# One start block with partition-ordered inputs, and routing sums by four column groups, in a two-expert-layer transformer kernel

## The reference, cut to what matters

```python
pooled = x.mean(axis=1)                 # x is the layer norm here; mean over 256 tokens
h = jnp.tanh(pooled @ W1 + b1)          # 128 -> 32
logits = h @ W2 + b2                    # 32 -> 8 zones
probs = softmax(logits); top_p, top_i = top_k(probs, 3)
...
z = gelu(x @ Wa[e]) @ Wb[e]             # Wa: 8 x 128 x 512, Wb: 8 x 512 x 128
return x + zone_outputs
```

## Time and profile before

| | us |
|---|---|
| median of 3 runs (lowest, highest) | 1666.61 (1665.81, 1667.47) |
| the profiled execution | 1665.73 |
| its span, first to last instruction | 1663.9 |
| `zones` "a" starts (first ACT instruction, L878) | 139.10 |
| `route` "b" starts (first PE instruction, L674) | 1024.73 |
| `zones` "b" starts | 1061.78 |

### The profile page before, as it was taken

One profiled execution on the slowest core, in us unless ns is written; L12 is line 12 of the kernel. 1 busy time (PEld: TensorE's weight loads), 2 busy tenths in 40 slices (PEclk: granted clock), 3 DMA queues, 4 the chain that ended last, 5 costly groups with the idle time before them and its releaser, 6 DMA issues. The chain is left out here.

```text
span 1663.9 us, 43913 instructions
## 1 busy us (share of the span) xinstructions
PE 1475.9 (89%) x14442; PEld 1086.5 (65%) x14443; DVE 1215.6 (73%) x2671; ACT 967.9 (58%) x1459; POOL 464.0 (28%) x672
## 2 busy tenths in 40 slices
PE   0068999998799999999999997899999979799797
PEld 0056999997456666666666656799999834499443
DVE  0755888887577887878778771388888879588695
ACT  0104666664366666666666653366666569677597
POOL 5032121211212222222222211121222168422386
PEclk9999999999799999999999997699999989899899
DMA  8000000000000000000000000000000000000011
GB/s 218 3 1 1 1 0 0 0 0 1 1 2 3 2 0 0 0 0 0 0 0 0 2 2 1 1 0 0 0 0 0 1 1 0 1 1 0 1 44 57
DMA packets 20585, 14.36 MB, mean 9 GB/s; under 512 B 7296, under 2 KB 16416, under 8 KB 20512
## 3 DMA queue, kind: packets, MB, share of 16 engines
q1 hardware_dynamic: 16008, 13.14, 2.8%
q10 hardware_dynamic: 3192, 0.15, 0.2%
q0 software_dynamic: 1312, 0.09, 0.1%
HBM read 9.18 MB, written 4.19 MB: 8 GB/s over the span
## 5 line engine op out<-in xcount | busy, mean ns | idle before, releaser
L1317 DVE TENSOR_REDUCE neg_max<-splat_fill_ps 128x2 f16<-128x512 f32 x512 | 333.8, 691 | 89.8 <-PE splat_fill_ps L1104 86.1
L1244 ACT ACTIVATE splat_probs<-splat_ring 128x1024 f32<-128x1024 f32 x256 | 248.1, 1021 | 98.1 <-PE splat_ring L1131 98.1
L889 ACT ACTIVATE zones_a_hidden<-zones_a_hidden_ps,gelu_scale 128x1024 f32<-128x1024 f32 x96 | 107.0, 1114 | 85.0 <-PE zones_a_hidden_ps L819 83.7
L1131 PE MATMUL splat_ring<-splat_queries,splat_keys 32*128 32x256 f32 x2048 | 152.7, 393 | 4.1 <-ACT splat_probs L1244 3.2
L889 ACT ACTIVATE zones_b_hidden<-zones_b_hidden_ps,gelu_scale 128x1024 f32<-128x1024 f32 x96 | 106.9, 1114 | 84.8 <-PE zones_b_hidden_ps L819 83.4
L1104 PE MATMUL splat_fill_ps<-splat_keys,splat_queries 32*128 32x256 bf16 x1024 | 146.2, 278 | 6.1 <-DVE neg_max L1317 3.2
L1145 PE MATMUL splat_mixed_ps<-splat_probs,values 128*32 128x256 f32 x2048 | 137.0, 385 | 0.4 <-ACT splat_probs L1244 0.4
L938 DVE SCALAR_TENSOR_TENSOR zones_a_hid_lo<-zones_a_hidden,unit_scale,zones_a_hid_hi 128x1024 f16<-128x1024 f32 x96 | 123.6, 1288 | 3.4
L938 DVE SCALAR_TENSOR_TENSOR zones_b_hid_lo<-zones_b_hidden,unit_scale,zones_b_hid_hi 128x1024 f16<-128x1024 f32 x96 | 123.6, 1288 | 3.4
L1131 PEld LDWEIGHTS splat_ring<-splat_queries,splat_keys 32*128 32x128 f32 x2048 | 99.6, 184 | 11.4 <-ACT splat_probs L1244 4.0
L817 PE MATMUL zones_a_hidden_ps<-zones_a_norm_hi,wa_hi 128*128 128x256 f16 x384 | 105.5, 275 | 0.3 <-DVE zones_a_norm_lo L928 0.3
(11 more groups left out here) (357 smaller groups left out, 3482.0 us busy)
## 6 DMA issues: line engine op xcount, KB each, us to landing
out<-x_res SPq DMA_DIRECT2D x16, 256.0 KB, 2.3
stage_a<-L_ffn_Wa SPq DMA_DIRECT2D x1, 2048.0 KB
qkv_rows<-L_attn_qkv_w SPq DMA_DIRECT2D x1, 192.0 KB
attn_w<-L_attn_W SPq DMA_DIRECT2D x1, 192.0 KB
deltas<-L_attn_splat_deltas ACTq DMA_DIRECT2D x6, 0.5 KB
log_scales<-L_attn_splat_log_scales POOLq DMA_DIRECT2D x6, 0.5 KB, 5.3
centers<-L_attn_splat_centers SPq DMA_DIRECT2D x6, 0.5 KB
log_amps<-ttn_splat_log_amplitudes SPq DMA_DIRECT2D x6, 0.5 KB
```

Source lines behind the costliest of these rows:

```text
L889: nc.scalar.activation(hidden[k][:, :, :], hidden_ps[of][:, :, :], ACT.Gelu_apprx_tanh, scale=s.gelu_scale[:, :]).then_inc(gelu_done, 1)
L1131: last = nc.tensor.matmul(ring[g // 2][:, 2 * (g % 2) + key_tile, :], keys[at][rows, t, key_tile * P:(key_tile + 1) * P], queries[at][rows ...
L1244: nc.scalar.activation(probs[u % PROB_BUFFERS][:, :, :, :].rearrange("p h k i -> p (h k) i"), ring[u % 2][:, :, :], ACT.Exp).then_inc(exp_ ...
L1317: nc.vector.tensor_reduce(s.neg_max[:, tile, t:t + 2, GROUP * g + SPLATS], fill_ps[f % 2][:, :, :], AX.X, ALU.max, negate=True).then_inc(m ...
```

## The change

The host now lays the inputs out by partitions: all small weights in one table of 128 rows of 1,680 f32 (0.86 MB), Wa and Wb as 128 rows of 16 KB each, x as 128 rows of 32 KB. Seven transfers, all from SP, replace the former ones: table, Wa, Wb, then x in four pieces. The four blocks in front of `route` "a", and its statistics and sums, become one block `start`. Constants `neg_max` and `values` are filled by POOL in place of DVE. The high parts of the weights are made by ACT (three passes over 4,096 columns), the low parts by DVE, but for a quarter of Wb's, which POOL makes.

The routing sums turn round: x streams (128 columns), and a 128 x 32 matrix that has `rstd` in the sample's own column and zeros elsewhere is the weight; tile n goes to the column group n mod 4, so that 32 rows of output per group collect 16 tiles. The four groups are added by a product with `own_spline` in `route`. For `route` "b" these sums stand at the end of `splat_attention`'s block, and POOL writes `rstd` to one more place per sample.

```diff
+def sum_rows(nc, s, out, samples):
+    for b in samples:
+        for t in range(TILES):
+            n = TILES * b + t
+            g = n % HEAD_GROUPS
+            last = nc.tensor.matmul(out[g * SAMPLES:(g + 1) * SAMPLES, :],
+                                    s.spread_rstd[:, t, SAMPLES * b:SAMPLES * (b + 1)], s.x_res[:, n, :],
+                                    start=(n < HEAD_GROUPS), stop=(n >= SAMPLES * TILES - HEAD_GROUPS))
+    return last
...
+            def _(sp):
...
+                sp.dma_start(s.packed[:, :], a["table"]).then_inc(packed_loaded, 16)
+                sp.dma_start(s.stage_a[:, :], a["wa"]).then_inc(a_loaded, 16)
+                sp.dma_start(s.stage_b[:, :], a["wb"]).then_inc(b_loaded, 16)
+                for n in range(PIECES):
+                    load_rows(n)
...
+            def _(pool):
...
+                nc.gpsimd.memset(s.spread_rstd[:, :, :], 0.0).then_inc(blank, 1)
+                nc.gpsimd.memset(s.neg_max[:, :, :, :], 0.0)
+                nc.gpsimd.memset(s.values[:, :, :, :, 0:SUM_COLUMN + 1], 1.0)
+                nc.gpsimd.memset(s.values[:, :, :, :, SUM_COLUMN + 1:GROUP], 0.0)
+                pool.wait_ge(blank, 1)
+                for n in range(PIECES):
+                    moments.power(pool, n)
+                    if n == 0:
+                        pool.wait_ge(high_ready, 1)
+                        nc.gpsimd.tensor_tensor(s.wb_lo[:, 0:LOW_SPLIT], s.stage_b[:, 0:LOW_SPLIT],
+                                                s.wb_hi[:, 0:LOW_SPLIT], ALU.subtract)
...
+                for n in range(PIECES):
+                    pe.wait_ge(moments.rstd_ready, n + 1)
+                    last = sum_rows(nc, s, sums_ps, range(n * SAMPLES // PIECES, (n + 1) * SAMPLES // PIECES))
+                last.then_inc(sums_done, 1)
...
+                act.wait_ge(scale_ready, 1)
+                nc.scalar.activation(s.stage_b[:, :], s.stage_b[:, :], ACT.Copy,
+                                     scale=scale[:, 1:2]).then_inc(scaled_ready, 1)
+                act.wait_ge(scaled_ready, 1)
+                nc.scalar.activation(s.wb_hi[:, :], s.stage_b[:, :], ACT.Copy).then_inc(high_ready, 1)
+                nc.scalar.activation(s.wa_hi[:, :], s.stage_a[:, :], ACT.Copy,
+                                     scale=scale[:, 0:1]).then_inc(high_ready, 1)
+                act.wait_ge(sums_done, 1)
+                nc.scalar.activation(s.sum_rows[:, :], sums_ps[:, :], ACT.Copy)
...
+                for n in range(PIECES):
+                    dve.wait_ge(x_loaded[n], 16)
+                    moments.statistics(dve, n)
+                dve.wait_ge(high_ready, 2)
+                nc.vector.scalar_tensor_tensor(s.wa_lo[:, :], s.stage_a[:, :], scale[:, 0:1], s.wa_hi[:, :],
+                                               ALU.mult, ALU.subtract)
+                nc.vector.tensor_tensor(s.wb_lo[:, LOW_SPLIT:], s.stage_b[:, LOW_SPLIT:], s.wb_hi[:, LOW_SPLIT:],
+                                        ALU.subtract)
...
 def route(nc, s, stage):
+                nc.tensor.matmul(pooled_ps[:, :], s.sum_rows[:, :], s.own_spline[:, :], start=True, stop=False)
                 pe.wait_ge(products_ready, 1)
...
 def splat_attention(nc, s, stage):
                 run(pe, slot)
+                pe.wait_ge(exp_done, HEAD_UNITS * SAMPLES)
+                for first, end in ((0, SAMPLES - 3), (SAMPLES - 3, SAMPLES)):
+                    pe.wait_ge(ended.ready, end)
+                    last = sum_rows(nc, s, ring[0][:, 0, 0:P], range(first, end))
+                last.then_inc(sums_done, 1)
...
                 run(act, slot)
+                act.wait_ge(sums_done, 1)
+                nc.scalar.activation(s.sum_rows[:, :], ring[0][:, 0, 0:P], ACT.Copy)
...
-                    nc.gpsimd.tensor_copy(s.rstd[:, columns], ended.rstd[at][:, :]).then_inc(ended.ready, 1)
+                    nc.gpsimd.tensor_copy(s.rstd[:, columns], ended.rstd[at][:, :])
+                    own = b * (SAMPLES + 1)
+                    own = slice(own, own + 1) if isinstance(b, int) else bass.ds(own, 1)
+                    nc.gpsimd.tensor_copy(s.spread_rstd[:, :, own],
+                                          ended.rstd[at][:, :].unsqueeze(2)).then_inc(ended.ready, 1)
```

More of the change, by code:

```diff
@@ new lines, with unpack @@
+PACKED_COLUMNS = sum(math.prod(shape) for _, shape in PACKED)
+def unpack(s, table):
+    at, parts = 0, {}
+    for name, shape in PACKED:
+        columns = math.prod(shape)
+        part = table[:, at:at + columns]
+        parts[name] = part if len(shape) == 1 else part.rearrange("p (a b) -> p a b", a=shape[0])
+        at += columns
+    s.qkv_rows, s.out_rows, s.centers, s.deltas = (parts[n] for n in ("qkv_rows", "out_rows", "centers", "deltas"))
+    s.log_scales, s.log_amps, s.movement, s.temperature = (
+        parts[n] for n in ("log_scales", "log_amps", "movement", "temperature"))
+    s.spline_bin, s.knot_b1, s.knot_w2, s.relu_scale = (
+        parts[n] for n in ("spline_bin", "knot_b1", "knot_w2", "relu_scale"))
+    s.wout4, s.spline_b2, s.win4 = (parts[n] for n in ("wout4", "spline_b2", "win4"))
+    s.bout_row, s.router_b2 = parts["bout_row"][0:1, :], parts["router_b2"][0:1, :]
+    s.router_w1, s.router_w2 = parts["router_w1"], parts["router_w2"][0:ROUTER_H, :]
+    s.router_b1 = parts["router_b1"][0:ROUTER_H, :]
+    s.attn1_w, s.attn1_bqk, s.attn1_bv = (parts[n] for n in ("attn1_w", "attn1_bqk", "attn1_bv"))
@@ L626, in power @@
         nc.gpsimd.tensor_tensor(s.rstd[:, columns], self.shifted[:, :],
-                                s.minus_half[:, 0:1].to_broadcast([P, self.tiles]),
-                                ALU.pow).then_inc(self.rstd_ready, 1)
-def route(nc, s, stage, few=0):
+                                s.minus_half[:, 0:1].to_broadcast([P, self.tiles]), ALU.pow).then_inc(self.powered, 1)
+        pool.wait_ge(self.powered, n + 1)
+        first, end = n * self.tiles // TILES, (n + 1) * self.tiles // TILES
@@ new lines, in power @@
+        nc.gpsimd.tensor_copy(s.spread_rstd[:, :, first * (SAMPLES + 1):(end - 1) * (SAMPLES + 1) + 1:SAMPLES + 1],
+                              s.rstd[:, columns].rearrange("p (b t) -> p t b", t=TILES)).then_inc(self.rstd_ready, 1)
+def sum_rows(nc, s, out, samples):
[7 more added lines that the diff above has]
+    return last
@@ L714, in _ @@
             def _(dve):
-                for n in range(parts if few else 0):
-                    moments.statistics(dve, n)
-                if few:
-                    dve.wait_ge(moments.rstd_ready, parts)
                 nc.vector.scalar_tensor_tensor(s.shift[:, :], s.mean[:, :], -1.0, s.rstd[:, :],
@@ L1877 @@
     nc = bacc.Bacc("TRN2", target_bir_lowering=False, num_devices=1)
-    arrays, aps = {}, {}
-    for name in INPUTS:
-        array = np.ascontiguousarray(inputs[name])
-        if array.ndim == 0:
-            array = array.reshape(1)
-        arrays[name] = array
+    arrays, aps = laid_out(np, inputs), {}
+    for name, array in arrays.items():
         aps[name] = nc.dram_tensor(name, array.shape, mybir.dt.from_np(array.dtype), kind="ExternalInput").ap()
```

634 lines of the change are left out of this document (284 added, 350 removed).

## The result

The changed kernel takes **1580.38 us** (median of four runs, 1579.62 to 1580.81); the kernel before took 1666.26 beside it. The ratio is 0.9483 with a 95% interval of 0.9467 to 0.9499. Forecast was 1583.

A forecast was written before the change was run, and what follows sets the result against it. Before 139 us the sum of serial stages was taken as the bound, then PE's router sums after the attention. 1665.73 - 61.0 - 22.4 = 1582.3, with 0.88 for the median 1583 us; range 1572 to 1597.

The forecast's parts named there:

- First data: Start: the table, the first transfer, lands and lets the DVE chain begin at 6.0 us, range 5.0 to 8.0.
- DVE chain: Start: splats 12.26, splines 5.14, maxima and scale 12.12, statistics 17.22 us at unchanged prices, ending at 52.8; POOL's fills cost 0.
- Transfers: Start: loads of Wa, Wb and x lie under the DVE chain and cost nothing, with 8 and 14 us of cover.
- ACT's high parts: Start: ACT's three passes end by 47.7 us, before DVE needs them at 52.8; costs nothing, 5 us of cover.
- The last piece and the low parts: End of start: DVE's low parts delay POOL's last `rstd` to 64.3; `route` begins at 67.05, all-ones products 61.0 us earlier.
- the standstill: End of start: POOL's first copy stands until Wa's low part ends, 57.3, its power until Wb's, 60.8; without it 67.1 gained.
- POOL is not held up: Rival, last piece of start: POOL works beside DVE's low parts or between them, DVE ends the block; 1577 us, chance 0.22.
- The end of the attention: Second router's sums: 116 passes at 52 ns, 6.0 us; all-ones products 22.4 us earlier, range 20.4 to 24.3.
- Bodies unchanged: Zones, attention and splines: bodies not touched and taken as they are, no change in length.
- groups work in turn: Rival, router's sums: column groups do not run at the same time; 14 to 25 us more, about 1600, chance 0.07.
- transfers pace the start: Rival, start: rows 16 and 32 KB apart load at half rate, 145 GB/s; 17 us more, 1600, chance 0.09.
- few engines serve the long rows: Rival, start: few of 16 engines carry the loads; with two, 36 GB/s, 1793 us, slower than before; chance 0.01.

The follow-up runs named there:

- the run in turn: Changed kernel with the router's sums ordered as 16 products for one column group, then 16 for the next, instead of alternating groups; 1591.51 us in one run.

## Why the prediction was right, and where it was not

The total came out 2.6 us under 1583, inside the range. In its own steps:

- **First data**: taken 6.0, was 5.12. The rate of the mean (5.0) was the better guide than the landing of a small transfer under load.
- **DVE chain**: splines 5.14 and 5.05, maxima and scale 12.12 and 12.10, statistics 17.22 and 17.22. Splats 12.26 and 12.90. Two errors meet there: the fills, taken as 0 with 1.5 as a bound, cost 1.45, and the chain without them is 11.45, since the pause for ACT that I used as their cover is gone. The upper bound was the price, and with it the rule that I had set beside it, the Trainium skill's (SBUF — State Buffer, section "SBUF: two separate sides"), by which a fill holds up a VectorE instruction in a two-port mode: the cast's row agrees with it, if the cast runs in such a mode, which no run shows.
- **Transfers**: nothing, as said: in the changed kernel DVE waits for a transfer once, at its first row, and with the old rows at 292 GB/s it waits no more. The cover was larger than the 8 and 14 us, as the rate was 424 and not 290.
- **ACT's high parts**: done at 45.93, predicted by 47.7 at the latest.
- **The last piece and the low parts**: the standstill carried over from the earlier trace rows is real. It fell on another instruction than I wrote. Not the last piece's power but the third piece's copy met Wa's low part, at 52.56, because POOL's pieces end close to DVE's. And POOL did not slip in between the two low parts. Whether a power in that place would have stood still is not shown; one that began before the low part did not. POOL's end was 63.85 for 64.3, the router's begin 66.44 for 67.05, and the all-ones products gained 61.7 for 61.0. The rival "POOL is not held up" (1577) is out: it took an edit to get there.
- **The end of the attention**: this term was mis-sized, 25.8 for 22.4, and beyond its range of 20.4 to 24.3 (its own bounds of 4.3 and 7.8 us give 20.6 to 24.1). The step that failed is "half the columns cost at the lower clock what all do at the higher", with 37 ns from the loads' row as the least. PE had no pause before these products, and the granted clock stayed at 1.00 from 960 to 965. A pass followed the other in 27 ns, loads included: 3.70 us to the end of all 128, where I had 6.8 with the last samples' share. In the start the same products last 421 ns each in place of 273, and their 32 loads take 1.48 us, 46 ns a pass (the granted clock reads 1.00 there, but the durations are longer). At that pace 116 passes would be 5.4 us, an estimate, near the 6.0 that I had. So the price fits the slower state, and the state was the mistake. The clock of the earlier trace rows had fallen while PE stood idle ahead of the old sums; the change took that idle time away. The estimate of 27 ns beside the Trainium skill's four times (TensorEngine Tiling (Array Packing), section "Theoretical Speedup") agrees with the row.
- **Bodies unchanged**: this is the step that I didn't work out. The table's two plus rows give back 2.85 us, which hid most of the tail's surplus; that the total came out so close is in part luck. In the second zones PE runs at the lower level for 4.9 us (977.5 to 982.4), where it did so for 2.5 before (1064.5 to 1067.0), but the zones are only 0.3 longer. With the old sums in front it is 2.7, with PE kept busy none; yet it is also 2.3 in the kernel without low parts, whose second router is that of the changed kernel, so the short router does not explain it. The 2.0 of the last splines go with the granted clock there. The block takes 106.0 again in the kernel without low parts, so the excess is no cost of the change that the runs would show. What decides when the clock comes up stays open, and so does the 0.95 in front; the attention's length drifts by more than that between kernels. POOL's extra copies (0.19 each) stayed within its waiting, 343.9 us in place of the 346.7 of the earlier trace rows.

The rivals in which groups work in turn, transfers pace the start, or few engines serve the long rows are excluded by the run in turn, by DVE's rows, which show no wait for a transfer behind the table, and by 424 GB/s at a DMA share of 0.99. That rate comes from rows 16 and 32 KB apart and is four times the 103 that the prediction sets beside this rival.

## What to carry to other kernels

When a chain of one engine is to become the bound, look at what that engine does after its last result: here two long two-input DVE instructions held POOL up, and moving them into pauses gave 7 us on top of the change. Products of 32 columns pay when neighbours in the queue go to different column groups (27 against 99 ns), and where a change removes idle time of PE in front of a stage, price the stage at both clock levels: here the granted clock stayed at 1.00 (960 to 965), where it had stood at 0.50 (1024.7 to 1052.0). Once a chain covers the loads, a faster layout buys nothing (1580.9 for 1580.4); don't credit it.

## What the runs showed that I had not expected

- POOL got no turn between two DVE instructions that follow each other without a wait: 7.53 us for a copy of 0.21, through 4.46 and 3.35. With DVE waiting for it after the first of the two, a copy ended 0.06 after that one (58.23 to 58.29).
- POOL's power of 2.9 us over 16 columns that began first ran beside DVE's two-input instruction with both at their usual length (2.90 and 4.36).
- A POOL fill, which only writes, held a DVE cast of three columns for 1.44 us; two reductions of 4.41 beside the same fills lost nothing.
- In the first zones PE stayed at the lower level although 14 products were put in front of them; in the second, the same 23 products gave the higher level in two profiled kernels and not in a third. No run here shows what decides it.
- Blocks without an edit differ between traces by more than some edits gain: the attention by 2.9 us and the last splines by 2.2.
